# A graph-network kernel on one core: ScalarE's loads of sorted edge groups take other places in its order during layer 2

## The reference, cut to what matters

```python
def _sage_conv(x, src, dst, W_l, b_l, W_r):          # network 0, twice (64 -> 128 -> 128)
    agg = segment_sum(x[src], dst) / max(count, 1)
    return agg @ W_l + b_l + x @ W_r
h = relu(_sage_conv(x, ...)); h = relu(_sage_conv(h, ...)); y = h @ W_out + b_out
x = layernorm(x + y)
# network 1: a message for every edge, summed by its second end
out = selu(concat(x[row], edge_attr) @ W1a + b1a) @ W1b + b1b
mean = segment_sum(out, col) / max(counts, 1)
y = selu(concat(x, mean, u[batch]) @ W2a + b2a) @ W2b + b2b
x = layernorm(x + y)
```

## Time and profile before

| | us |
|---|---|
| median of three runs | 2545.67 |
| the profiled execution's own time | 2547.18 |
| its span | 2545.4 |
| TensorE, matmuls, busy | 2084.5 (82%) |
| GpSimd busy | 1845.8 (73%) |
| VectorE busy | 1637.0 (64%) |
| ScalarE busy | 1015.8 (40%) |

### The profile page before, as it was taken

The page is one execution under the profiler, slowest core; times in us unless marked ns, Lnnn a source line. Parts: engine busy times, 40 slices in busy tenths (PEclk is TensorE's granted clock), DMA queues, the critical chain, the costliest instruction groups (busy, mean ns, idle before and its releaser), DMA issues. The chain is left out here.

```text
span 2545.4 us, 54296 instructions
## 1 busy us (share of the span) xinstructions
PE 2084.5 (82%) x19234; PEld 1539.5 (60%) x19234; DVE 1637.0 (64%) x3320; ACT 1015.8 (40%) x2319; POOL 1845.8 (73%) x1864
## 2 busy tenths in 40 slices
PE   1899999989989998984788888888878888867753
PEld 1555565555545555553676676777767777766753
DVE  6899999996455564554566666666666666643433
ACT  3787877874000000013344344444433444433322
POOL 5546768676777777777777777777777777777775
PEclk9999999999999999985899999998999999986665
DMA  8368786777769877824433333333333333332212
GB/s 298 111 231 224 228 264 180 250 198 134 210 208 253 237 210 232 241 59 109 123 74 74 71 80 74 77 76 72 76 77 74 80 74 74 72 71 51 51 41 46
DMA packets 524456, 342.56 MB, mean 135 GB/s; under 512 B 398996, under 2 KB 476495, under 8 KB 520781
## 3 DMA queue, kind: packets, MB, share of 16 engines
q1 hardware_dynamic: 407075, 267.01, 38.2%
q0 software_dynamic: 54240, 57.31, 10.3%
q10 hardware_dynamic: 62890, 14.87, 2.9%
HBM read 201.55 MB, written 137.36 MB: 133 GB/s over the span
## 5 line engine op out<-in xcount | busy, mean ns | idle before, releaser
L987 POOL DMA_INDIRECT A_sb<-source_terms,src_cur x1092 | 1049.1, 961 | 332.9 <-issue 327.4
L938 POOL DMA_INDIRECT sorted_edges<-pm_row,pm_to x520 | 575.4, 1107 | 183.6 <-issue 154.1
L1871 DVE TENSOR_TENSOR arena<-iota_code,arena 128x2048 f16<-128x2048 f16 (+1 forms) x392 | 435.5, 1179 | 19.6 <-PE cnt_ps L1416 17.3
L1082 ACT ACTIVATE A_sb<-cnt_ps 128x392 f32 (+1 forms) x784 | 383.8, 499 | 135.9 <-PE cnt_ps L1416 86.2
L1545 PE MATMUL agg_ps<-A_sb,arena 128*128 128x448 f16 x1911 | 378.6, 355 | 0.0
L1416 PEld LDWEIGHTS cnt_ps<-arena 128*128 128x128 f16 x3136 | 191.1, 100 | 225.7 <-issue 161.4
L1416 PE MATMUL cnt_ps<-arena 128*128 128x98 f16 x3136 | 280.3, 214 | 44.5 <-ACT A_sb L1082 27.1
L1545 PEld LDWEIGHTS agg_ps<-A_sb,arena 128*128 128x128 bf16 x1911 | 186.1, 99 | 165.0 <-issue 5.3
L1647 PE MATMUL agg_ps<-A_sb 128*65 128x48 f32 x2184 | 179.5, 243 | 123.1 <-DVE A_sb L2208 123.1
L1647 PEld LDWEIGHTS agg_ps<-A_sb 128*65 128x65 f32 x2184 | 165.7, 158 | 138.4 <-DVE A_sb L2208 130.4
L1423 PE MATMUL agg_ps<-A_sb,arena 128*65 128x448 f16 x686 | 243.3, 355 | 0.0
(11 more groups left out here) (308 smaller groups left out, 3505.7 us busy)
## 6 DMA issues: line engine op xcount, KB each, us to landing
counts_matrix<-A_sb SPq DMA_DIRECT2D x12, 5488.0 KB, 17.4
A_sb<-counts_matrix SPq DMA_DIRECT2D x12, 5488.0 KB, 18.7
arena<-in_edge_attr_dram SPq DMA_DIRECT2D x90, 256.0 KB
sorted_edges<-zrow SPq DMA_DIRECT2D x13, 1716.0 KB
arena<-sorted_edges SPq DMA_DIRECT2D x169, 128.0 KB
A_sb<-source_terms,src_cur POOLq DMA_INDIRECT x1092
overlapping_rows<-A_sb SPq DMA_DIRECT2D x1, 13056.0 KB, 39.4
pm_row<-in_edge_attr_dram ACTq DMA_DIRECT2D x46, 256.0 KB
```

Source lines behind the costliest of these rows:

```text
L938: pool.indirect_dma_start(out=sorted_d, out_offset=bass.IndirectOffsetOnAxis(ap=pm_to[:, k, j:j + 1], axis=0), in_=pm_row[:, k, j, :], in_ ...
L987: pool.indirect_dma_start(out=gath[k][:, j * F:(j + 1) * F], out_offset=None, in_=p_d, in_offset=bass.IndirectOffsetOnAxis(ap=src_cur[k][: ...
L1082: act.activation(Asb(half)[:, :, bass.ds((b * BG + k) * GROUP, GROUP)].rearrange("p b (w j) -> p b w j", j=PAIR), cnt_ps[k % 2][:, 0:SUB * ...
L1871: ins = dve.tensor_tensor(hot_rows[:, slots], iota_code[:, 0:n, :].unsqueeze(1).to_broadcast([P, AT_ONCE * SUB // 2, n, 2]), turned[:, bas ...
```

## The change

It moves calls of `load_group` in ScalarE's layer 2 code, and changes nothing else.

```diff
                 if not isinstance(m, int) or m < NSB - 1:
                     act.wait_ge(hT_turned, m + 1)
                     act.activation(hTs[:, :], t_ps[:, 0:SBN], ACT.Copy).then_inc(hT_moved, 1)
-                if s is not None and (s == 1 or LAYER2[s - 1] == 4):
-                    load_group(FIRST[s] + 2)
                 act.wait_ge(h2_turned, m + 1)
                 act.activation(h2T, t2_ps[:, 0:SBN], ACT.Copy).then_inc(h2_moved, 1)
                 if s is not None:
-                    load_group(FIRST[s] + 3)
+                    load_group(FIRST[s] + LAYER2[s] - 1)
                 act.wait_ge(var_ready, m + 1)
                 act.activation(st[:, 3, :], st[:, 2, :], ACT.Sqrt, bias=eps_t[0:CH, 0:1], scale=1.0 / F).then_inc(std_ready, 1)
+                if s is not None:
+                    load_group(FIRST[s + 1])
                 act.wait_ge(x2_turned, m + 1)
                 act.activation(x2T, cnt_ps[1][0:F, 0:SBN], ACT.Copy).then_inc(x2_moved, 1)
                 act.activation(x2all[:, bass.ds(at, 1), :, :].rearrange("p a c f -> p (a c) f"), x2c[:, :, :], ACT.Copy).then_inc(x2_kept, 1)
                 if s == NSB - 1:
                     act.wait_ge(hT_turned, NSB)
                     act.activation(hTs[:, :], t2_ps[:, 0:SBN], ACT.Copy).then_inc(hT_moved, 1)
                 if s is not None:
-                    load_group(FIRST[s] + 4)
+                    load_group(FIRST[s + 1] + 1)
+                    if s + 1 < NSB and LAYER2[s + 1] == 4:
+                        load_group(FIRST[s + 1] + 2)
                     move_agg2(s)
-                    load_group(FIRST[s] + 5)
```

## The result

The changed kernel took 2557.86 us (median of 20 runs, 2544.48 to 2564.78), the kernel before 2546.88 us on the same occasion (20 runs, 2542.22 to 2553.99). The ratio is 1.0038, with a 95% interval of 1.0024 to 1.0052: slower by some 10 us. The forecast was 2553.9 us in a range of 2542.0 to 2558.5.

A forecast was written before the change was run, and what follows sets the result against it. GpSimd was taken to bound the edge stage and nearly layer 2; late TensorE blocks would delay the first gather. Adding 8.2 us to the 2545.67 us median gave 2553.9 us, range 2542 to 2558.5.

The forecast's parts named there:

- GpSimd bounds layer 2 once nothing starves it, and the edge stage: Edge stage lasts what GpSimd needs, 1382 us; in layer 2 GpSimd was nearly a bound, starving 4.2 us.
- the 5.7 us: Most that could be gained before the first gather: 4.2 us of GpSimd starving and 1.5 us for the stores.
- Load 27 meets the counts load: End of block 1: load waits for scatter 22, is held till 715.8, and the sums move 15.7 us late.
- Block 2 opens: Start of block 2, 0.6 us after the late move of the sums, at 716.4.
- The clock's 1.5 us: TensorE's matmuls after a long wait: the lower clock costs 1.5 us more.
- GpSimd starves before group 25: GpSimd in layer 2: the scatter starts at 727.0 and not 724.47, starving 2.5 us.
- Load 37 free: Load 37 wants scatter 32, landed at 811.2; it is due at 813.9, so no cost.
- Block 7: End of block 7: load 47 goes 1.6 us ahead of the counts load, not held; block 8 starts 2.0 us late.
- rival 2: Load 47 is already held at block 7; sums end 6.4 us late, 2552.1 us; chance 0.22.
- Block 10: End of block 10: load 57 waits for scatter 52, is held till 1032.0, and block 11 starts at 1032.6.
- rival 1: No hold at block 10; the first gather comes 3.0 us sooner, 2542.7 us; chance 0.15.
- The sums end: End of layer 2's last block: 1132.6 instead of 1124.40, 8.2 us late.

The follow-up runs named there:

- experiment 1: Changed kernel with SyncE's counts load issued only after ScalarE's move of the sums; 2540.32 us, ratio 0.9986 to the kernel before.
- experiment 2: Changed kernel with the fourth load (groups 27, 37, 47, 57) put behind the move of the sums; 2547.56 us, ratio 1.0010 to the kernel before.

## Why the prediction was right

I compare by the time behind the first zeroing matmul (668.13 before, 674.04 after), since stage 1 isn't part of the change.

- **GpSimd bounds layer 2 once nothing starves it, and the edge stage.** Right: experiment 1, without any starving, gives the 5.7 us that the prediction had as 4.2 and 1.5. That it comes out to the tenth is partly chance: 0.74 us of waiting for the stores are left there, and counted from scatter 22 the gain is 5.3 us.
- **Load 27 meets the counts load.** Right in kind, one term mis-sized: the scatter's landing. I let scatter 22 land 1.3 us behind its last issue. That holds where no counts load is in flight (1.4 us in experiment 1). After, it took 712.99 - 708.63 = 4.4 us, with the counts load issued 0.35 us before that issue ended, and the scatter's last packets stood behind the first large ones of the counts load. The load went 4.7 us behind the counts load and not 2.3. It made no difference, since the counts load sets when the held DMA is let go: 722.12 - 708.28 = 13.8 us, and I had taken 13.5.
- **Block 2 opens 48.3 us behind the first zeroing matmul** by the prediction, 48.7 measured. The clock's 1.5 us were 5.80 - 4.13 = 1.7 in the 21 matmuls.
- **GpSimd starves before group 25.** Predicted from 726.7 on, 58.9 us behind the first matmul; measured 59.7. It starved 4.5 and not 2.5 us: the slot came 0.8 us later, GpSimd came to it 0.9 us sooner, and 0.3 of the 4.5 is the usual gap.
- **Load 37 free.** Right: there TensorE doesn't wait.
- **Block 7: load 47 ahead of the counts load, not held.** Right, and so rival 2 was wrong in this execution. It led by 2.5 us and not 1.6; block 8 opened 0.9 us late and not 2.0.
- **Block 10: load 57 held.** Right, and rival 1 wrong in this execution, but by a margin of 0.4 us, so that this branch came and not rival 1 is in part luck. The hold is the term that was mis-sized most: let go 1034.73 - 1024.78 = 9.95 us behind the counts load, against 13.5. The load went 0.4 us behind the counts load, where 1.1 was predicted. Block 11 opened 361.3 us behind the first matmul, predicted 364.5. The 1.5 us of clock were 2.5: block 11 took 1070.05 - 1035.37 = 34.7 us instead of 32.1.
- **The sums end** 462.4 us behind it, predicted 464.5; before it was 456.3. So 6.1 us late and not 8.2.
- **First gather** 484.3 us, predicted 485.9: 6.6 us later than before and not 8.2. The stores were awaited 2.16 us instead of 1.51. GpSimd starved before groups 25, 55 and 64, the three that were named.

The sum was 2553.9 and the median came out at 2557.9. The part of the change that the profile shows is smaller than forecast (6.6 for 8.2), and the whole larger (9.7 by the ratio). The difference lies in stage 1, or in runs unlike the profiled one. So the mechanism was right in the profiled execution, and that the median still fell within 4 us of the forecast owes something to luck: the sum had 1.6 us too much in layer 2, mostly by a hold that was 3.6 us too long in it, and the measured time has some 3 to 4 us that no term of the sum stands for.

Two more points on the prediction as it stands. It named as a sign of being wrong that the length from first to last gather changes; it did, from 1382.0 to 1378.3 us, but the experiments at this pace have 1377.8 and 1377.5, so this is the profile of the kernel before and not the change. And its upper bound, 2558.5, is too low for what it names: two holds of 15.7 us instead of 13.5 and two clock losses of 2.8 us instead of 1.5 add 2 x 2.2 + 2 x 1.3 = 7.0 us, which gives 2560.9. The measured median lies 0.6 us under the bound as recorded.

**Which runs were which.** The changed kernel's 20 runs fall into two heaps: 5 at 2544.5 to 2548.6 us and 15 at 2554.5 to 2564.8 (two of the expectations above say 6 and 14, which is a miscount). The forecast at block 10 hung on 1.1 us, and rival 1 (load 57 just ahead of the counts load) lay 11 us below it. The heaps would fit that, but the only profile at this pace is from the upper heap, so this is argued and not shown. Against it speaks experiment 2: there load 57 stands behind the move of the sums and wasn't held in the profile, and the 12 runs still lie in two heaps, 5 and 7, with 5 us between them. The heaps may have another cause.

**A rule beside the row.** The trace has load 47 going out 2.5 us ahead of the counts load and its third DMA taking 0.45 us. By the Trainium skill (DMA: Bandwidth & Descriptors, Queues, rings and completion order) an engine rotates between queues packet by packet, so what is drained by then can't be slowed, and what isn't is. The case agrees on both sides of the edge, and so do its DMA records: scatter 22's last 16 packets went by 712.7, behind the first packets of 44 KB, and while the third DMA was held ScalarE's queue got 44 packets to the counts load's 64. What the rule doesn't give is when the held DMA is let go: that was 13.8 us behind the counts load's issue in one block and 9.95 us in another, while most of the load's bytes had still to move, and what sets it stays open.

## What to carry to other kernels

A small load issued within a few microseconds behind a bulk load held its own engine's queue for 7 to 12 us here; what counts then is which instruction is queued behind it. Moving loads to take away three waits (18.7 us together) brought two of 27.2 us, because the load stood ahead of the only instruction that the next block could not start without, and it waited for a buffer. The cure that worked best was not in that queue: the bulk load can be made to wait for the move. A few microseconds are also hard to read from one profile: where GpSimd stands when layer 2 begins moved by 2 us between executions, and experiment 2 has the earliest first gather in its profile but not the best median.

## What was not expected of the hardware

- The landing of a scatter is itself delayed by a bulk load issued at the same time: 4.4 us against 1.3 to 1.4. This was seen once, in the changed kernel's block 1, with the packets above beside it; at block 10, where the counts load was issued 0.9 us behind the scatter's end, it landed in 1.3 us.
- The hold's length isn't one number: 13.8 and 9.95 us from the counts load's issue in the same kernel. Both lie well before the load's own end, which comes 18.6 us behind its issue by the view of DMA issues of the kernel after (times, KB each, median us from issue to landing):

```profile
A_sb<-counts_matrix SPq DMA_DIRECT2D x12, 5488.0 KB, 18.6
```

- The same programs took 40% longer on three of the four occasions of the experiments, with the same duration of each gather but 10 us stands between groups of them, and there a change worth 5 us at the usual pace was worth nothing.
